# Two attention stages and a ternary layer merged into one program, with the row maximum as bias of exp and one of four low parts moved to GpSimd

## What is computed

```
x = x + tanh(g_xattn[0]) * L0_xattn(_layernorm(x), ctx, mask)
x = x + tanh(g_ffn[0])   * L0_ffn(_layernorm(x))
x = x + tanh(g_xattn[1]) * L1_xattn(_layernorm(x), ctx, ctx)
x = x + tanh(g_ffn[1])   * L1_ffn(_layernorm(x))
```

```
x = einsum('bdn,bdm->bnm', Q, K) / sqrt(128)    # 512 x 512 scores of one tile
out = einsum('bvn,bnm->bvm', V, sigmoid(x))
```

## Time and profile before

| what | us |
|---|---|
| median of 3 runs | 1336.06 (1332.77 to 1338.27) |
| the profiled execution: its time | 1338.2 |
| the profiled execution: its span | 1336.5 |
| PE busy / DVE / ACT / POOL | 1224.6 / 712.1 / 551.9 / 433.5 |
| Heads, from the first instruction to the last | 0 to about 470 |
| Features | about 470 to 582.6 |
| Experts | 582.9 to the end |

### The profile page before, as it was taken

How to read it: one execution, slowest core, us unless ns; L and a number is a source line. 1 busy time by engine, 2 the same in 40 slices (tenths; PEclk the granted TensorE clock), 3 DMA queues, 4 the chain that set the end, 5 groups by cost and what they waited for, 6 DMA issues and landing times. The chain is left out here.

```text
span 1336.5 us, 26105 instructions
## 1 busy us (share of the span) xinstructions
PE 1224.6 (92%) x7848; PEld 1029.7 (77%) x7849; DVE 712.1 (53%) x1401; ACT 551.9 (41%) x1362; POOL 433.5 (32%) x521
## 2 busy tenths in 40 slices
PE   6998999999897579959999999899999999999995
PEld 5876777778776357745677777789999888899995
DVE  5667556556556479974466664643224553424241
ACT  4544445345345168853221111443334553434342
POOL 1102211210211365551002664234444434444433
PEclk9999999999999779979999999999999999999998
DMA  9100000000000021132100131476445566555554
GB/s 329 31 17 19 17 1 19 17 1 18 1 1 2 0 64 39 46 123 96 57 0 1 65 129 40 153 184 144 78 78 135 143 178 153 138 94 129 85 137 71
DMA packets 54907, 101.36 MB, mean 76 GB/s; under 512 B 5158, under 2 KB 22054, under 8 KB 54838
## 3 DMA queue, kind: packets, MB, share of 16 engines
q0 software_dynamic: 15824, 37.76, 14.9%
q1 hardware_dynamic: 39014, 62.70, 14.4%
HBM read 73.96 MB, written 26.48 MB: 75 GB/s over the span
## 5 line engine op out<-in xcount | busy, mean ns | idle before, releaser
L1873 PE MATMUL t_H<-m_W,t_xT 128*128 128x352 f32 x1632 | 281.5, 328 | 7.3 <-DVE m_W L1951 5.8
L1873 PEld LDWEIGHTS t_H<-m_W,t_xT 128*128 128x128 f32 x1632 | 262.9, 189 | 10.0 <-DVE m_W L1951 8.2
L1841 POOL DMA_INDIRECT out_dram<-t_ys,t_sid x68 | 109.5, 1610 | 223.8 <-ACT t_ys L1902 107.7
L1918 ACT ACTIVATE t_sl<-t_H 128x352 f32<-128x352 f32 x68 | 31.5, 463 | 174.9 <-PE t_H L1873 174.9
L601 ACT ACTIVATE pr<-pr 128x128 f32<-128x128 f32 x256 | 76.1, 298 | 55.3 <-DVE pr L762 54.0
L66 PE MATMUL t_Y<-m_W,t_hT 128*128 128x512 f32 (+1 forms) x207 | 88.1, 426 | 5.0 <-issue 3.1
L1996 DVE TENSOR_TENSOR t_hT<-t_TH,t_hT 128x384 fp32r<-128x384 f32 x68 | 37.8, 556 | 101.6 <-ACT t_hT L1939 100.5
L1972 DVE TENSOR_TENSOR t_h<-t_H,t_sl 128x352 f32<-128x352 f32 x68 | 35.6, 524 | 103.5 <-ACT t_sl L1918 103.5
L1902 ACT ACTIVATE t_ys<-t_Y,t_wcol 128x512 f32<-128x512 f32 x69 | 47.2, 685 | 94.7 <-PE t_Y L68 94.7
L68 PE MATMUL t_Y<-m_W,t_hT 128*128 128x512 f32 (+1 forms) x207 | 82.1, 397 | 0.0
L67 PE MATMUL t_Y<-m_W,t_hT 128*128 128x512 f32 (+1 forms) x207 | 81.9, 396 | 0.0
(11 more groups left out here) (446 smaller groups left out, 3278.2 us busy)
## 6 DMA issues: line engine op xcount, KB each, us to landing
m_raw<-in_L_ffn_w_dram SPq DMA_DIRECT2D x28, 704.0 KB, 5.9
m_raw<-in_L_ffn_w_dram SPq DMA_DIRECT2D x14, 512.0 KB, 4.1
aCX<-in_ctx_dram SPq DMA_DIRECT2D x20, 256.0 KB, 2.6
rows_d<-before_w SPq DMA_DIRECT2D x17, 256.0 KB, 2.0
CT<-in_ctx_dram SPq DMA_DIRECT2D x8, 512.0 KB, 3.7
X<-in_x_dram SPq DMA_DIRECT2D x4, 1024.0 KB, 12.6
out_dram<-X SPq DMA_DIRECT2D x3, 1024.0 KB, 4.3
m_raw<-in_L_ffn_sw_dram SPq DMA_DIRECT2D x4, 704.0 KB, 5.8
```

The source lines that it names most:

```text
L1841: pool.indirect_dma_start(out=m["out_rows"][:, :], out_offset=bass.IndirectOffsetOnAxis(ap=sid[:, b:b + 1], axis=0), in_=ys[:, b, :], in_o ...
L1873: x_ = pe.matmul(bk[b % 2][:, 0:I], xT[:, b % 2, jx, k, :], W13[:, jw, k, j, :], start=k == 0 and jx == jw, stop=k == KC - 1 and jx == 1)
```

## The change

`attention_and_ternary` replaces both attention functions. Heads and Features are one list now, with no barrier between them, no loop and static addresses.

1. **Softmax.** DVE still takes the maximum, then makes a 128x4 tile `neg` from it; the 128x512 subtraction is gone. ACT's `exp` reads the PSUM bank and takes `neg` as a bias. The bank is released by the last `exp` (`p_exp`) instead of by the subtraction (`s_out`), and the sums are clamped ahead of the reciprocal.
2. **One list.** The last group of Heads has a text of its own: the gate's projection `g` comes earlier, `oP.2` stands behind the last scores, and the first steps of Features (`an`, `qh`, `ks`, `aT`, `aS`, `ag`) are woven in. Then follow 64 steps `m` of Features, and the ternary layer's last two tiles with all their steps are hung between the first 21 of them.
3. **Low parts.** The low part of a tile's second score row is made by POOL, `ag` with n = 1.
4. **Statistics.** Those of 12 of the 16 tiles for Experts are made inside the 64 steps (`ta.2`, `ta.3`), so that its first norms wait for nothing; the gate's transposes stand behind the first two tiles.
5. The three scores, and the norms and splits of two tiles, that the old loop made in vain behind the last tile are gone. The buffers of Features lie in the dead weights of Heads, so names in the trace change: `Wk` holds k and q, `Wq` the sigmoids, `kT` their float32 copy, `Wv` v.

```
+        for m in range(MS):
+            b, n = m // KC, m % KC
+            text = [between.get(m, "")]
+            if m + 3 < MS:
+                text += [f"aS.{(m + 3) // KC}.{(m + 3) % KC}"]
+            if m + 2 < MS:
+                text += [f"ag.{(m + 2) // KC}.{(m + 2) % KC}"]
+            if n == 0 and b + 2 < NB:
+                text += [f"an.{b + 2}"]
+            if n == 2 and 1 <= b + 1 < NB and b:
+                text += [f"aT.{b + 1}"]
+            text += [f"ap.{b}.{n}" if n < KC - 1 else f"aO.{b}"]
+            if n == KC - 1 and b + 2 < NB:
+                text += [f"qh.{b + 2} ks.{b + 2}"]
...
+            plan += steps(" ".join(text), NG)
...
+                    elif kind == "ag" and s[2] == 1:
+                        pool.wait_ge(as_hi, KC * t + 2)
+                        pool.tensor_tensor(as_[:, 1, 1, :], asg[:, 1, :], as_[:, 1, 0, :].bitcast(F32), ALU.subtract).then_inc(as_low, 1)
+                    elif kind == "ks":
...
+                            pool.wait_ge(as_fill, KC * (t - 1))
+                        pool.tensor_copy(ak[:, t % 2, 0, :], aCX[t % GB]).then_inc(ak_hi, 1)
+                        pool.wait_ge(ak_hi, t + 1)
+                        pool.tensor_tensor(ak[:, t % 2, 1, :], aCX[t % GB], ak[:, t % 2, 0, :].bitcast(F32), ALU.subtract)
+                        pool.wait_ge(aq_hi, t + 1)
+                        pool.tensor_tensor(aq[:, t % 2, 1, :], axn[:, t % 2, :], aq[:, t % 2, 0, :].bitcast(F32), ALU.subtract)\
+                            .then_inc(aq_lo, 1)
...
+                    elif kind == "aS":
+                        n, m = s[2], KC * t + s[2]
+                        if n == 0:
+                            pe.wait_ge(aq_lo, t + 1)
...
                     elif kind == "sm":
...
-                        dve.tensor_tensor(pr[:, t % 2, :, :], bk, mx[:, t % 2, :].unsqueeze(2).to_broadcast([P, HQ, S]),
-                                          ALU.subtract).then_inc(s_out, 1)
+                        wait(dve, p_exp, t - 1)
+                        dve.tensor_scalar(neg[:, t % 2, :], mx[:, t % 2, :], MASKED / 10, -SCALE0, ALU.max, ALU.mult).then_inc(s_out, 1)
...
-                            i = act.activation(pp, pp, ACT.Exp, scale=SCALE0, accum_out=sums[:, t // HQ % 2, at_:at_ + 1])
+                            at_ = t % HQ * HQ + slot
+                            i = act.activation(pr[:, t % 2, slot, :], SC[t % 2][:, slot * S:(slot + 1) * S], ACT.Exp, scale=SCALE0,
+                                               bias=neg[:, t % 2, slot:slot + 1], accum_out=sums[:, t // HQ % 2, at_:at_ + 1])
```

More of the change, by code:

```diff
@@ L91, in program, with row_scale @@
             parts[f"passed_{e}"] = top.enter_context(nc.semaphore(f"passed_{e}"))
-        attention_heads_and_ternary(nc, parts, x, g_x, g_f, fw, fb, ctx_in, mask, norm_w, wq, wk, wv, wo, wg)
-        attention_features(nc, parts, ctx_in)
+        attention_and_ternary(nc, parts, x, g_x, g_f, fw, fb, ctx_in, mask, norm_w, wq, wk, wv, wo, wg)
         experts(nc, parts, gate_w, ebias, w1, w2, w3, sw1, sw2, sw3, out)
[L97 to L104, removed]
+def row_scale(dve, c, done, tiles, eps):
+    t, bst, mean = c["tmp16"][:, :, tiles], c["bst"][:, tiles, :], c["mean"][:, tiles]
+    diff, squares, var, r1 = (t[:, k, :] for k in range(4))
+    n = 0
     def step(*instrs):
@@ L118, in row_scale, with row_power, attention_and_ternary @@
     step(dve.scalar_tensor_tensor(out=var, in0=squares, scalar=1.0 / D, in1=r1, op0=ALU.mult, op1=ALU.add))
[L119 to L145, removed]
+    dve.tensor_scalar(t[:, 4, :], var, eps, None, ALU.add).then_inc(done, 1)
+def row_power(pool, c, done, tiles, powered):
+    pool.wait_ge(done, 7)
+    pool.tensor_tensor(c["rstd"][:, tiles], c["tmp16"][:, 4, tiles], c["nhalf"][:, tiles], ALU.pow).then_inc(powered, 1)
+def attention_and_ternary(nc, c, x, g_x, g_f, fw, fb, ctx_in, mask, norm_w, wq, wk, wv, wo, wg):
     X, identF = c["X"], c["identF"]
@@ L1236, in _, with gate @@
             def _(pe):
-                pe.wait_ge(g_in, 32)
-                for k in range(KC):
-                    i = pe.transpose(G[:, k * E:(k + 1) * E], gw[:, k * P:(k + 1) * P], c["identF"][0:E, 0:E])
-                i.then_inc(gt, 1)
-                pe.matmul(L[:, 0:E], c["onesF"][0:1, :], b1[:, :], start=True, stop=True).then_inc(bias_ps, 1)
+                def gate():
+                    pe.wait_ge(g_in, 32)
+                    for k in range(KC):
+                        i = pe.transpose(G[:, k * E:(k + 1) * E], gw[:, k * P:(k + 1) * P], c["identF"][0:E, 0:E])
+                    i.then_inc(gt, 1)
+                    pe.matmul(L[:, 0:E], c["onesF"][0:1, :], b1[:, :], start=True, stop=True).then_inc(bias_ps, 1)
                 def logit(g):
```

378 lines of the change are left out of this document (179 added, 199 removed), and 8 rows, old and new, of the table d.

## The result

| kernel | median of its runs, us | lowest to highest |
|---|---|---|
| before, beside it on the same chip | 1337.16 (4 runs) | 1332.77 to 1338.72 |
| the changed kernel | 1358.37 (4 runs) | 1357.08 to 1360.15 |

The change makes the kernel slower: the ratio is 1.0164, 95% interval 1.014 to 1.0188. The forecast was 1362. The profiled execution took 1357.76 us, its span is 1356.1, so between the two spans 19.6 us are to be explained.

The account below looks back on a forecast made before the run. PE was taken to bound Heads, PE and DVE to share the bound in Features. -38.6 + 66.3 - 1.8 = +25.9 on the profiled 1338.2 gives 1364.1; that execution being 2.1 above the median, 1362 us was forecast, range 1338 to 1377.

Parts of the forecast that it names:

- The mechanism: Features: POOL's in-order queue puts the new low part ahead of the next split, so PE idles about 3 us per tile.
- Rival A: Features: POOL's low part is ready early enough, PE bounds at 6.1 us a tile, 1295 us in all; chance 0.12.
- The cycle: Features, first score of one tile to the next: 10.9 us against 6.16 before; fourteen lose 66.3 us.
- The part of the clock: Features: PE's lower clock level after idle pieces stretches 9.4 us a tile to 9.4 to 11.9; 10.9 taken.
- Rival B: Features: POOL's chain binds but the full clock holds, 9.1 to 9.5 us a tile, 1337 to 1342 us; chance 0.14.
- t(1): First score of tile 1 in Features: forecast at 445.0 us against 483.56 before, 38.6 us gained.
- each of the four shrinks by 1.0: Heads: PE's four 2.8 us waits for the quantiser each shorten by 1.0 through the new softmax, 4.0 us in all.
- the seam: Between Heads and Features: merging the stages was put at a gain of 28.5 us here.
- the last group: End of Heads: projections moved under waits take back 2.8 us of waiting and 1.6 of lower clock.
- The `exp`: Heads: the bias from a tile adds 0.09 us to each of 256, hidden beside other work on ACT.
- The end of Features and Experts: After tile 15's first score: 1.8 us gained in Features; the start of Experts costed at nothing, 0 to 3 gained.
- Costed at nothing: First six cycles of Features: the last two tiles' ternary steps, 10 us on POOL and 3 on PE, fall into POOL's idle time.

Follow-up runs that it names:

- POOL's order alone: The changed kernel with POOL making the split of tile T ahead of the low part of tile T-1's second score row: 1317.7 us, ratio 0.985.
- the kernel with the filler: The changed kernel plus twelve unused matmuls on PE ahead of its wait for the split, in tiles 2 to 15: 1347.18 us, ratio 1.0067.

## Why the prediction was right, point by point

**The mechanism** was as stated, at its place and with its releaser: 14 idle pieces of PE, each ended by POOL's low part of q, four POOL operations without a gap, 5.7 us of waiting for ACT's sigmoid, a granted clock of 0.83 over the cycles (0.75 to 0.9 were named). That moving POOL's one operation, or the split by one step, takes away 41 and 47 us shows it by experiment. Rival A, that the cycle would not bind, is refuted for this order. It is what the kernel with the split one step earlier does (6.0 a cycle in the middle); with POOL's order alone the cycle is still 6.9.

**The cycle:** 10.66 measured, 10.9 predicted, 9.1 and 11.9 the ends. The chain alone was put at 9.4 at the full clock; it is 9.39 in the one cycle that kept it, and 9.5 with the idle time filled. The part of the clock was put at 1.5 a cycle; over the last eight cycles it is 1.4 (10.91 less 9.49). What the sum of fourteen had wrong is the first cycle, which is 8.34: of the 3.3 us that the cycles came out shorter, 2.6 are there. The terms on POOL differ from what was read. The low part of q takes 1.71 instead of 1.28 to 1.46 in 9 of the 14 cycles, those in which it begins while a low part on DVE is still at work (512.22 to 513.71 in the cycle shown at the end), and 1.26 in four; that of k takes 1.27 instead of 1.52 in most. In the cycle shown the two errors cancel to 0.1, which is luck. The prediction had put the 1.52 down to DVE's norm; the rows at the end put such waits down to DVE's low part. Rival B asked for a held clock: the kernel with the filler has it, and at 1347 lies 5 above that rival's range; in the change 12 of 14 cycles had a stretch at the lower level.

**t(1):** 442.3 instead of 445.0. The sum was right within 3 us, its terms were not. The softmax was put at 4.0 + 1.7; the run with the old softmax puts it at 11.8 of t(1). The step that failed is "each of the four shrinks by 1.0": those in groups 1 to 3 did, from 2.77 to 1.73, and the fourth did not (2.81 to 2.93). But three waits of 1.0 to 1.1 ahead of the quantiser's second transposes, not among the terms, vanished altogether (at 167.25, 270.43 and 372.29 in the kernel with the old softmax), and three of 0.5 shrank to 0.3. A sum over the waits of one length missed the shorter ones. These and the 1.3 us that the lower clock cost behind the wait at 234 make some 8 of the 11.8; the rest was not followed up. What remains of the gain, 29.5 (483.56 to 454.08 with the old softmax), is the merging: it had been put at 28.5 for the seam and 4.4 for the last group, 3.4 too much.

**The `exp`:** 80 ns more each, 90 predicted, and 29 more on the read of its accumulator, which I hadn't listed. Both lie in ACT's idle time, as costed: ACT is busy 215 of 418 us in Heads. On DVE the 64 subtractions of 44.3 us in all became operations of 12.0, the 32 us less that were forecast; the busy time of the stretch fell by only 16.3, because steps of Features and more of the last group stand in it now (it is 253.0 with the old softmax in the same list).

**The end of Features and Experts:** gains of 1.3 and 0.9 where 1.8 and 0 (0 to 3) were predicted, the 0.9 within the spread of Experts; ACT's first weights wait for their load, as forecast.

**Costed at nothing:** the ternary steps inside the first cycles. With the chain in place that is what they cost. The figure beside it, "if the cover failed they would cost up to 6 us", is wrong: with the chain gone they cost 14.5, in cycles in which DVE is busy 95% of the time (42.9 of 45.0 us). This never showed in the forecast's number but it is why the three expectations of kernels without the chain were 13 to 14 us too low.

**The total:** 1362 against 1358.4. The 25.9 of the sum became 19.6: 2.7 less from t(1), 3.3 less from the cycles, 0.9 from Experts, and 0.5 more from the end of Features. That t(1) came so close is luck in part: its softmax term was 6.1 too small and its merging term 3.4 too large.

## What to carry to other kernels

An operation given to an idle engine is priced by what its queue holds behind it, not by the engine's busy share: POOL was busy half the time, and a 1.3 us operation put one place too early cost 47 us, where at its right place it gave some 4 at most. Draw the chain from an event of one round to the same event of the next through every in-order queue; if it is longer than the busiest engine's work, nothing else matters, and a swap of two neighbours in the list may cure it. When a chain like that goes, what it had covered becomes visible, so sum each engine's work afresh for the stretch that gets shorter.

## What the runs showed of the hardware that was not expected

DVE's low parts (two inputs in SBUF) became longer, a mean of 1001 ns, where L849 took 692 before, though there are fewer. The timeline of DVE has the reason in one cycle:

```profile
512.22 1.49 DVE L838 TENSOR_TENSOR Wq<-kT,Wq 128x512 fp32r<-128x512 f32 x1
513.63 1.48 DVE L825 TENSOR_SCALAR xn<-X,mean,rstd 128x512 f32<-128x512 f32 x1
515.03 0.68 DVE L838 TENSOR_TENSOR Wq<-kT,Wq 128x512 fp32r<-128x512 f32 x1
517.00 0.69 DVE L838 TENSOR_TENSOR Wq<-kT,Wq 128x512 fp32r<-128x512 f32 x1 [1.29 <-ACT Wq L692]
```

The one at 512.22 begins while POOL's low part of k is at work (511.89 to 513.16) and takes 1.49 us, while POOL's takes its 1.27; the two that begin when POOL is done take 0.68 and 0.69. Before, it was the other way round. DVE's low part came first there, and POOL's took longer:

```profile
520.93 0.67 DVE L849 TENSOR_TENSOR as<-asg,as 128x512 fp32r<-128x512 f32 x1
521.07 1.68 POOL L879 TENSOR_TENSOR ak<-aCX,ak 128x512 fp32r<-128x512 f32 x1 [0.18 <-POOL ak L877]
```

In both traces it is the one that begins second that gets longer. Of the low parts that the traces list singly, 17 in the changed kernel begin inside a `TENSOR_TENSOR` of 128x512 on POOL and take 1.21 to 1.78 us, and the other 28 take 0.67 to 0.69; before, one begins so. The Trainium skill (SBUF - State Buffer, Who interferes with whom) says that a DVE instruction with two SBUF inputs contends with a GpSimd instruction that reads SBUF; these rows agree, and here it is mostly DVE that pays, where the prediction had thought of POOL. With POOL working through a quarter of the low parts, this is part of what fills DVE in the cycles of the ternary steps: with the split one step earlier the mean is 1013 ns, and 887 when POOL makes none. How much of the 14.5 us it makes was not measured by itself.

The clock fell in 12 of the 14 cycles, behind idle pieces of 1.6 to 3.6 us, and was at the full level again later in the same cycle (1.00 from 519.5 to 523.5). The length of the piece alone does not decide: behind one of 1.63 (461.40) the cycle had 0.85, behind one of 1.84 (472.30) it kept 1.00, and in Heads pieces of 2.8 were followed by the lower level only twice in four times. What decides was not tried.
